# Gate chunk loads one step sooner, and five row buffers in place of three, in a fused convolution and expert kernel

## The reference, cut to what matters

```python
x = x + conv(ln_c(x))          # (16, 64, 56, 56); a 7x7 filter made anew for every pixel
t = to_tokens(x)               # 50176 tokens of 64 channels
n = ln_t(t)
logits = n @ Wg + bg           # 8 experts
top_w, top_i = top_k(logits, 2); top_w = softmax(top_w)
t = t + sum over the two experts e of top_w[e] * (gelu(n @ W1[e] + b1[e]) @ W2[e] + b2[e])
return from_tokens(t)
```

## Time and profile before

| | us |
|---|---|
| median of 3 runs (2396.77 to 2417.44) | 2416.89 |
| the profiled execution | 2408.16 |
| its span | 2406.4 |
| PE busy | 1961.1 (81%) |
| DVE busy | 1501.7 (62%) |
| POOL busy | 937.3 (39%) |
| ACT busy | 841.2 (35%) |

### The profile page before, as it was taken

One profiled execution on the slowest core, in us unless ns is written; L12 is line 12 of the kernel. 1 busy time (PEld: TensorE's weight loads), 2 busy tenths in 40 slices (PEclk: granted clock), 3 DMA queues, 4 the chain that ended last, 5 costly groups with the idle time before them and its releaser, 6 DMA issues. The chain is left out here.

```text
span 2406.4 us, 34530 instructions
## 1 busy us (share of the span) xinstructions
PE 1961.1 (81%) x10208; PEld 1212.0 (50%) x10208; DVE 1501.7 (62%) x2687; ACT 841.2 (35%) x1540; POOL 937.3 (39%) x977
## 2 busy tenths in 40 slices
PE   4992888997989999998999985308898889988934
PEld 3761444444545455555555545306666666666623
DVE  2441665665878878787788876625666556666623
ACT  2540111111222213222122223206666666666700
POOL 6000000000234332343323437755777777777720
PEclk9995998999999999999999995559999999999955
DMA  7768777777777777777777733138888888888658
GB/s 224 159 134 179 178 192 184 177 189 187 208 193 203 213 199 190 199 211 202 194 193 199 197 95 110 54 99 245 255 251 246 244 245 249 250 251 242 212 161 267
DMA packets 291481, 474.18 MB, mean 197 GB/s; under 512 B 120156, under 2 KB 196059, under 8 KB 268327
## 3 DMA queue, kind: packets, MB, share of 16 engines
q1 hardware_dynamic: 258055, 439.69, 68.0%
q0 software_dynamic: 28832, 30.65, 4.6%
q10 hardware_dynamic: 4416, 1.73, 0.3%
HBM read 392.67 MB, written 81.93 MB: 197 GB/s over the span
## 5 line engine op out<-in xcount | busy, mean ns | idle before, releaser
L954 POOL DMA_INDIRECT token_rows<-gate_rows,gate_index x392 | 412.7, 1053 | 980.4 <-DVE gate_index L1273 866.7
L1153 DVE TENSOR_TENSOR prod<-z_ps,r_all 119x896 f32<-119x896 f32 x512 | 545.2, 1085 | 184.4 <-PE z_ps L1066 159.0
L1485 POOL DMA_INDIRECT mixed<-exp_mix,exp_xt x474 | 483.9, 1021 | 215.0 <-issue 134.6
L1070 PE MATMUL z_ps<-xq,band 112*119 112x448 f32 x1024 | 440.9, 568 | 37.5 <-DVE prod L1153 37.4
L1508 ACT ACTIVATE exp_hid<-exp_h_ps,exp_pack 128x384 f32<-128x384 f32 x632 | 331.8, 579 | 21.7 <-PE exp_h_ps L1552 20.1
L1552 PE MATMUL exp_h_ps<-exp_tok,exp_pack 128*128 128x384 f32 x1264 | 272.3, 359 | 65.5 <-issue 60.0
L1070 PEld LDWEIGHTS z_ps<-xq,band 112*119 112x119 f32 x1024 | 186.1, 190 | 245.2 <-issue 182.6
L1552 PEld LDWEIGHTS exp_h_ps<-exp_tok,exp_pack 128*128 128x128 f32 x1264 | 221.1, 194 | 162.1 <-issue 156.4
L986 ACT ACTIVATE ob<-o_ps 128x448 f32<-128x448 f32 x64 | 34.9, 545 | 623.0 <-PE o_ps L1083 623.0
L1564 PE MATMUL exp_y_ps<-exp_hid,exp_pack 128*64 128x384 f32 x1264 | 242.8, 506 | 0.0
L1083 PE MATMUL o_ps<-prod,pick 119*32 119x448 f32 x2048 | 241.2, 564 | 0.9 <-DVE prod L1153 0.3
(11 more groups left out here) (194 smaller groups left out, 2130.7 us busy)
## 6 DMA issues: line engine op xcount, KB each, us to landing
xq<-xs SPq DMA_DIRECT2D x192, 896.0 KB
exp_pack<-packs SPq DMA_DIRECT2D x316, 321.5 KB
exp_xt<-token_rows SPq DMA_DIRECT2D x158, 120.0 KB
xs<-xpad SPq DMA_DIRECT2D x32, 448.0 KB, 5.7
xin<-in_x_dram SPq DMA_DIRECT2D x8, 1568.0 KB, 11.4
co<-ob SPq DMA_DIRECT2D x512, 24.5 KB
merge_yt<-mixed SPq DMA_DIRECT2D x28, 448.0 KB, 5.0
mixed<-exp_mix,exp_xt POOLq DMA_INDIRECT x474
```

Of the source, the lines that this page charges most:

```text
L954: pool.indirect_dma_start(out=token_rows[:, :], out_offset=bass.IndirectOffsetOnAxis(ap=index[b % RR][:, j:j + 1], axis=0), in_=rows[b % R ...
L1070: mm = nc.tensor.matmul(zt, band[t % BR][rows_in, at:at + MF], maps, start=True, stop=True)
L1153: nc.vector.tensor_tensor(prod[(NU * t + u) % PR][:, :, :].rearrange("p m (d x) -> p m d x", d=D), z_ps[(NU * t + u) % 3][0:MF, :, 0:CN].r ...
L1485: pool.indirect_dma_start(out=mixed[:, :], out_offset=bass.IndirectOffsetOnAxis(ap=xt[t % XT][:, j, ROW_ID:ROW_ID + 1].bitcast(U32), axis= ...
```

## The change

`load_chunk` is called in SP's iteration t for the chunk of step t+1, where it was called for that of step t. Its place within the iteration, behind the stores, stays. The rings of `gate_rows` and `gate_index` have five buffers each and not three, with as many semaphores.

```diff
-    XR, PR, BR, XC, SQ, RR = 8, 6, 3, 3, 2, 3
+    XR, PR, BR, XC, SQ, RR = 8, 6, 3, 3, 2, 5
...
                 if 0 <= t - 2 < STEPS:
                     store(t - 2)
-                if t in chunk_at:
-                    load_chunk(chunk_at[t])
+                if t + 1 in chunk_at:
+                    load_chunk(chunk_at[t + 1])
```

## The result

The changed kernel takes 2417.96 us in the median of 16 runs (2407.54 to 2427.53), the kernel before, run beside it, 2405.07 (16 runs, 2395.69 to 2417.44). The ratio is 1.0046, with a 95% interval from 1.0027 to 1.0066: some 11 us slower (the medians lie 12.9 apart), where 15 us faster was forecast. The forecast of 2402 was taken from 2416.89, the median of the first three runs; from 2405.07 the same 15 us would have given 2390, so the miss is 26 to 28 us and not the 16 between 2402 and 2417.96. All ratios here are of undisturbed executions alone: a few, of 2582 to 7752 us, are left out of them. The profiled execution after took 2411.59 us with a span of 2409.6.

A forecast was written before the change was run, and what follows sets the result against it. SP's DMA queue, as good as full all the time, was taken as the bound. 8.7 - 2.4 - 3.6 + 12.7 = 15.4 us sooner gave 2402 against the median of 2416.89, range 2384 to 2415, chance 0.60.

The forecast's parts named there:

- SP's passes: SP's loop from band 19 to band 63: 832.7 us in place of 841.4 when left free, 8.7 us less.
- the chunk in front: Band 63, like every other in a quarter, has one chunk more ahead of it on SP: 2.4 us lost.
- slack of the strips: At the convolution's end PE can move up 12.7 us before it waits for strips: step 63's strip lands early.
- the added wait: A quarter's first chunk waits on SP for stores just issued: 1.2 us, three times, 3.6 us lost.
- The slower rival: SP stands for stores landing behind 2.8 MB of strips: 35 us, result 2433, deciding from 6.3 us per landing; chance 0.12.
- The other bound: For the three store landings ahead of a quarter's first chunk: a strip's 11.8 us each, 35 us in all.
- PE's waits: PE's chunk waits during the convolution, 59.8 us plus 2.43 of step 62, go; wall time only as SP's loads allow.
- Ring of five: ACT's 57.7 us of waits for scatters in the tail go, worth nothing, as POOL's row has no gap.
- the signs of being wrong: Band of step 63 before 1350, SP pausing over 3 us before a quarter's first chunk, or scatters shorter than 160 us.
- The rival of PE as the bound: PE sets the pace and SP's queue only follows: all chunk waits won, 87 us, result 2330; chance 0.09.
- A page against the row: Skill page's 358 GB/s from HBM against the profile's 198: a pass of 19.05 us would take 10.5, the queue no bound.

The follow-up runs named there:

- the changed kernel without the wait: Changed kernel, but each quarter's first chunk reads x twice and not co, so it waits for no store: 2406.69 us, ratio 1.0006 to the kernel before.
- the wait alone: Kernel before, with SP waiting at the end of iterations 17, 33 and 49 until that quarter's stores have landed, no load moved: 2411.93 us, ratio 1.0027.
- the split band: Each step's filter band loaded by two DMAs, of 112 and 7 rows, not one of 119: kernel before 2264.29 us (0.9403), changed kernel 2265.13 (0.9402).
- the one with the first chunks put back: Changed kernel, but the first chunk of each quarter is loaded in its old iteration: 2403.65 us, ratio 0.9993 to the kernel before.
- the kernel with less PE work: Kernel before without one of PE's three products on the first strip (high band, low part of the maps): 2403.57 us, ratio 0.9985.
- half strips: Half of every strip's bytes left out from the ninth strip on: kernel before 2280.49 us (0.9479), changed kernel 2267.89 (0.9427).

## Why the prediction was wrong

The sum has four terms. Measured are, from single traces, the kernel before against the changed kernel without the wait (first three rows), and this one against the changed kernel (fourth row); us, faster is positive, the sum rounded last.

| | forecast | measured |
|---|---|---|
| SP's passes | +8.7 | -7.8 |
| the chunk in front | -2.4 | -3.9 |
| slack of the strips | +12.7 | +8.1 |
| the added wait | -3.6 | -6.4 |
| sum | +15.4 | -10.1 |

Two steps failed. The gain of the earlier chunks, the first three terms, was put at 19 us and is nothing: by the medians the kernel without the wait has the ratio 1.0006 [0.9984, 1.0028]. That is the larger part of the miss, and of it SP's passes are the largest term. And the added wait was priced at 1.2 us per landing where it was 7.5; this one made the kernel slower and not merely no faster.

**The added wait.** The prediction took 1.2 us per landing, from a row where the queue was idle. Measured: 7.60, 7.74 and 7.15. By the medians the wait costs 11.3 us (2417.96 and 2406.69), half of the pauses' length, and not 3.6; in the kernel before the wait alone costs 5 of 23.4 us. The slower rival had this mechanism, its place, and a point of decision of 6.3 us, and the landings lie above it; it was given 0.12. Its arithmetic was no better, though: 22.5 us of pauses turn 15.4 + 3.6 into 3.5 us slower, and the 11 came about because the pauses cost half as much and the gain was missing. The argument "SP comes to the chunk only once the queue has taken all stores" doesn't carry: that an issue has been taken says nothing of when it lands. The other bound, a strip's 11.8, was the nearer row.

What the 7 us consist of the packets show. After the change, at the first pause (526.42 to 534.02), the view of DMA from 529 to 533 us is this:

```profile
DMA  1001002000100100100100100100000000000000
DMA packets 83, 0.09 MB, mean 22 GB/s; under 512 B 74, under 2 KB 74, under 8 KB 74
```

Nine rows of strips, one in each 0.3 us, and then the last rows of the stores: the last four of the 7.60 us are the one late engine again. With the split band the pauses are as long, for another reason: SP's stores are issued by 476.26 and the queue still moves strips ahead of them, so that from 478 to 482 us all is busy:

```profile
DMA packets 1093, 0.77 MB, mean 194 GB/s; under 512 B 1023, under 2 KB 1023, under 8 KB 1023
```

**SP's passes.** Forecast 832.7 us from band 19 to band 63, against 841.4. The changed kernel without its wait needed 849.2, the one with the first chunks put back 845.4. The prediction had two thirds of the 26.4 us of waits given back; all of it was: over 690 us (560 to 1250) the kernel before moved 199 GB/s, the changed one 196. I read it so that a pause on SP in the kernel before had cost the queue next to nothing, because the DMA engines still had work queued; no run tests this by itself. Why the passes even became a little longer is open. This term was worth -4 to -8 us, not +8.7.

**The chunk in front** was forecast at 2.4 us. Without the wait band 19 comes at 331.6 us, 3.9 later than before: right in kind, a little small.

**Slack of the strips.** Forecast 12.7 us; band 63 to the last copy fell from 58.4 to 50.4, so 8.0. The landing of step 63's strip was right (issue ended at 1390.4, taken at 1403.07, 12.7 us). The need was wrong by one user: the prediction took DVE's low part, but ACT's `gate_std` stands behind the split on ACT, and DVE and then PE wait for it. ACT ended the split at 1404.98, DVE began on the low part at 1410.02, and those 5 us are about what was missing.

**PE's waits** for chunks went, as forecast, and ACT's waits for strips spread (77.5 us in 33 waits). **Ring of five:** worth nothing, as forecast (ratio 1.0000), with a tail of 165.0 us and memsets that end at 204.95. Of the signs of being wrong one came, a pause of more than 3 us on SP; the scatters' start, expected near 1423, stayed at 1439.50.

**The rival of PE as the bound** is ruled out by the kernel with less PE work and those with half strips, and the reading of SP as held back by its queue was right. But "the queue is full" was taken as a rate that cannot be changed, with the 0.78 share of the earlier trace rows as a leftover. **A page against the row:** the estimate of 10.5 us per pass was set aside as neither shown nor ruled out. The idle quarter that the text named held the finding: for 15% of the time a single packet was under way.

## What to carry to other kernels

A load that is moved sooner moves its waits too: price the wait by a landing in the full queue at that place, counted from the end of the issue, and name what stands behind it. When an engine is freed by an earlier load, ask first whether the queue has time to give; taking out compute and taking out bytes, one kernel each, answers it. And a full queue with DMA engines that are only three quarters busy is a question, not a bound: look at it in slices of a tenth of a microsecond for a load that runs on one engine, and split its rows so that both sides' outermost dimension divides by 16, as the strips' did here.

## What the runs showed of the hardware

- A load of 119 rows (17 x 7) of 952 bytes had at most two packets under way and took 5.5 to 8.5 us, at 16 to 19 GB/s where it ran by itself; as 112 and 7 rows it took a median of 0.78 us, cost 0.56 and 0.48 us to issue, and the kernel became 142 us faster (6%), the clock's part included.
- Stores of 24.5 KB queued behind 2.8 MB of strips landed 7.1 to 8.3 us after their last issue, against 1.2 us at 1440 us, where no strips were queued.
- With PE waiting for nothing its clock was 1.00 from 300 to 480 us (2.4 GHz throughout); in the kernel before, where PE was busy 159 of these 180 us, it was 0.92.
- Pauses on SP of 7 to 8 us cost nothing that can be measured where the queue had slack, and between a fifth and a half of their length where it was full. The strip behind one was issued in 1.24 us and not in some 4.
